# Gathering the next expert unit's rows ahead of sending the finished unit's rows, in a fused attention and mixture-of-experts block

## The chip, the cores and the metric

The kernel is one launch on 1 core of a Trainium2 chip. The metric is device time in microseconds, the median of several executions. The profile shows one execution; in it PE is the TensorE matmul, PEld its weight load, DVE is VectorE, ACT is ScalarE, POOL is GpSimd and SP is SyncE, which here only issues DMAs.

## What is computed

Sixteen sequences of 100 tokens, each of 512 numbers, go through a gated cross-attention with a causal mask and then through a layer of 8 experts, of which each token uses one:

```python
x = x + tanh(g_xattn[0]) * attention(layernorm(x), ctx_512, Wq, Wkv_expand, Wout)
xn = layernorm(x).reshape(-1, 512)
route = sigmoid(xn @ router_w)
max_ind, max_prob = argmax(route, axis=1), max(route, axis=1)
for e in range(8):
    h = silu(xn @ gate_w[e]) * (xn @ up_w[e])
    y = y + where(max_ind == e, h @ down_w[e], 0.0)
x = x + tanh(g_ffn[0]) * (y * max_prob)
```

`gate_w` and `up_w` are 8 x 512 x 1024, `down_w` is 8 x 1024 x 512, all float32. Each float32 product is made of three matmuls on split operands (high part times high part, low times high, high times low).

## The kernel before, in words

The program is written engine by engine: each engine has a block of its own with a fixed order of instructions, and semaphores tie the blocks together. Nothing reorders an engine's instructions; a wait holds up all that stands behind it on that engine.

The first half (up to about 265 us) is attention, in four chunks of 400 tokens, with the routing of each chunk's tokens. It leaves three tables in HBM: `x2_rows`, the normalised rows that the experts read; `x1_rows`, the rows before the expert layer with each token's scale beside them; and `token_table`, which lists for each expert which tokens are its own.

The second half is the expert loop. Its step is a *unit*: up to 256 tokens (`CAP`) of one expert. In the profiled execution there are 8 units, numbered 0 to 7, one for each expert. For one unit:

- GpSimd reads the unit's token numbers from `token_table` into `idx_next` and gathers those rows of `x2_rows` into the tile `xg` by two indirect DMAs of 128 rows (`gather_next`, lines 541 to 546, with the gathers themselves in `gather_tokens`, line 536). `xg` is the memory of the tile `x2`, so the trace shows it as "x<-x_rows,idx_next".
- PE turns the rows (`turn_tokens`, transposes on line 1401: 8 matmuls for a unit) into PSUM, ACT and DVE split them into `x_hi` and `x_lo`. DVE's `x_lo` step counts up the semaphore `g_lo_done`.
- The width of 1024 is worked on in four steps (j from 0 to 3). In each, `gate_up` makes 48 matmuls of 256 columns and `down` 12 of 512 columns (the lines of all of them are 1147 to 1149, the three products of the helper `three`; a gate or up matmul is named "bank<-x_hi,gu_hi" and a down matmul "bank<-wq_hi,wkv_hi", since those buffers are used again).
- SP loads each step's weights (line 407, three DMAs of 512 KB for gate, up and down) into `staging`, which has room for two steps; ACT makes the high parts (`gu_hi`, line 611), DVE the low parts (`gu_lo`, line 780), into buffers for two steps.
- GpSimd reads the token numbers again, into `idx_now`, and gathers the rows of `x1_rows` (`gather_now`, lines 548 to 556). DVE scales the experts' result and adds it to these rows (`finish`, line 1116, tile `rows`, shown as "xn"; semaphore `rows_done`).
- GpSimd scatters the rows to the output (`send_rows`, line 562) with the indices in `idx_now`, and `wait_sent` waits until they have landed before `gather_now` may write `idx_now` anew.

PE's order sets the frame. In its loop iteration u it does gate_up(u,1), down(u,0), gate_up(u,2), down(u,1), turn_tokens(u+1), gate_up(u,3), down(u,2), gate_up(u+1,0), down(u,3). `turn_tokens(u+1)` waits for the gather of unit u+1. DVE does the split of unit u+1's tokens after gate_up(u,3), and `finish(u)` after its step for gate_up(u+1,0).

GpSimd's order in iteration u is send_rows(u), gather_next(u+2), wait_sent(u), gather_now(u+1). So the rows of unit u+2 are asked for when unit u is finished. Before it loads the indices, `gather_next(.., u+2)` waits until `g_lo_done` says that unit u+1's tokens are split, since `xg` has one buffer. `gather_next` for unit 1 stands ahead of the loop; the loop covers units 2 to 7, which is six gathers.

Of the kernel before, what the change touches and what calls it, by code (L numbers as in the profile page):

```python
# [71 lines left out]
def flamingo_block(nc, x, ctx, g_xattn, g_ffn, Wq, Wkv, Wout, router_w, gate_w, up_w, down_w, out):  # L72
    B, S, H = x.shape
    L = ctx.shape[2]
    E, _, I = gate_w.shape
    HD = 32
    NH = H // HD
# [35 lines left out]
    with st:  # L113
# [313 lines left out]
        def _(pool):  # L427
# [106 lines left out]
            def gather_tokens(u):  # L534
                for t in range(TT):
                    nc.gpsimd.indirect_dma_start(xg[:, t, :], None, x2_rows,
                                                 bass.IndirectOffsetOnAxis(ap=idx_next[:, t:t + 1], axis=0),
                                                 bounds_check=T - 1, oob_is_err=False).then_inc(xg_loaded.sem, 16)

            def gather_next(base, u):  # L540
                pool.wait_ge(g_lo_done.sem, g_lo_done.after(u, 0))
                nc.gpsimd.dma_start(idx_next[:], token_table[bass.ds(base, CAP), :].rearrange("(p t) o -> p (t o)", p=P)
                                    ).then_inc(idx_next_loaded.sem, 16)
                pool.wait_ge(idx_next_loaded.sem, idx_next_loaded.after(u - 1, 16))
                pool.sem_inc(wait_passed, 1)
                gather_tokens(u)

            def gather_now(base, u):
                nc.gpsimd.dma_start(idx_now[:], token_table[bass.ds(base, CAP), :].rearrange("(p t) o -> p (t o)", p=P)
                                    ).then_inc(idx_now_loaded.sem, 16)  # L550
                pool.wait_ge(idx_now_loaded.sem, idx_now_loaded.after(u, 16))
                pool.sem_inc(wait_passed, 1)
                for t in range(TT):
                    nc.gpsimd.indirect_dma_start(x1g[:, t, :], None, x1_rows,
                                                 bass.IndirectOffsetOnAxis(ap=idx_now[:, t:t + 1], axis=0),
                                                 bounds_check=T - 1, oob_is_err=False).then_inc(x1g_loaded.sem, 16)

            def send_rows(u):
                for t in range(TT):
                    pool.wait_ge(rows_done.sem, rows_done.after(u, t + 1))  # L560
                    pool.sem_inc(wait_passed, 1)
                    nc.gpsimd.indirect_dma_start(of, bass.IndirectOffsetOnAxis(ap=idx_now[:, t:t + 1], axis=0),  # L562
                                                 rows[:, t, :], None, bounds_check=T - 1,
                                                 oob_is_err=False).then_inc(rows_sent.sem, 16)

            def wait_sent(u):
                pool.wait_ge(rows_sent.sem, rows_sent.after(u, 16 * TT))
                pool.sem_inc(unit_sent.sem, 1)

            def first_slot(u):  # L570
                return pool.value_load(units[0:1, bass.ds(u * 2 + 1, 1)], min_val=0, max_val=slot_max)
# [21 lines left out]
            gather_next(first_slot(1), 1)  # L593
            gather_now(0, 0)
            with pool.Fori(0, more + (E - 2)) as u:
                send_rows(u)
                gather_next(first_slot(u + 2), u + 2)
                wait_sent(u)
                gather_now(first_slot(u + 1), u + 1)
            last = more + (E - 1)  # L600
# [880 lines left out]
```

## Time and profile before

| what | value |
|---|---|
| times of three executions | 595.16, 594.67, 589.15 us; median 594.67 |
| span of the profiled execution, first to last instruction | 593.0 us; its own device time isn't listed apart from the three times above |
| busy share of the span | PE 89%, PEld 75%, DVE 60%, ACT 52%, POOL 31% |
| granted TensorE clock, mean | 0.952 of full speed |
| DMA | 77.31 MB, 130 GB/s on average |

How to read it: the span is shorter than a device time, because what lies before the first and behind the last instruction isn't in it. The ends of matmuls are modelled, so that one matmul's shown duration overlaps the start of the next; the distance from one start to the next is the better measure of what it costs. "[2.33 <-DMA ...]" behind a row is the idle time of that engine before it and what ended it.

### The profile page before, as it was taken

What the parts mean: (1) busy time and instruction counts of PE and PEld (TensorE: products, weight loads), DVE (VectorE), ACT (ScalarE), POOL (GpSimd) and SP (SyncE); (2) the same over time, 40 slices, a digit from 0 to 9 for tenths busy, and PEclk for the clock granted to TensorE, in tenths of its full rate; (3) what the DMA queues carried; (4) which work ended last, traced back from release to release, by engine and by line L of the source; (5) the groups of instructions that cost most, each with busy time, mean ns of one, the idle gap of its engine ahead of it and who ended that gap; (6) DMA issues with size and microseconds to landing.
All of it is one profiled execution on the core that took longest, in us unless ns stands there. A gap on an engine that the chain in (4) does not pass through costs nothing.

```text
span 593.0 us, 11407 instructions
## 1 busy us (share of the span) xinstructions
PE 527.9 (89%) x3724; PEld 446.4 (75%) x3724; DVE 354.3 (60%) x745; ACT 307.5 (52%) x855; POOL 181.1 (31%) x210
## 2 busy tenths in 40 slices
PE   1999999999899999765999899898997997989991
PEld 1966786587658765555899799797997997979981
DVE  3677579557855576873557557475464563755641
ACT  1898659745974795221445535355353443544520
POOL 5544226315631463325311213112124041121111
PEclk9999999999999999955999999999898998999996
DMA  8400121221120310724475656657377366474620
GB/s 208 141 1 2 52 75 58 70 78 48 43 69 14 85 53 21 257 83 99 136 240 176 218 176 213 228 173 222 113 240 249 122 186 225 156 224 134 239 65 27
DMA packets 58910, 77.31 MB, mean 130 GB/s; under 512 B 5398, under 2 KB 40830, under 8 KB 58880
## 3 DMA queue, kind: packets, MB, share of 16 engines
q1 hardware_dynamic: 53728, 66.90, 36.2%
q0 software_dynamic: 5152, 10.03, 5.5%
q8 instruction: 15, 0.25, 0.2%
q14 instruction: 15, 0.12, 0.1%
HBM read 68.81 MB, written 10.86 MB: 134 GB/s over the span
## 4 chain that ended last, share of the span: by engine, by line
PE 51%; DMA 13%; issue 11%; DVE 8%; ACT 7%; POOL 5%; POOLq 2%; DVEq 1%; ACTq 0%; SPq 0%
PE bank L1147 13%; PE bank L1148 13%; PE bank L1149 13%; DMA x<-x_rows,idx_next 7%; DMA idx_next<-token_table 4%; ACT pr L667 3%; POOL pn L507 2%; PE bank L1242 2%; PE bank L1232 2%; PE bank L1401 2%; POOL out_x L562 2%; DMA staging<-in_L_xattn_Wq 2%; PE bank L1281 1%; ACT wq_hi L611 1%; PE bank L1168 1%
## 5 line engine op out<-in xcount | busy, mean ns | idle before, releaser
L1147 PE MATMUL bank<-x_hi,gu_hi 128*128 128x256 f32 x512 | 147.8, 289 | 2.9 <-ACT qT L743 1.5
L1148 PE MATMUL bank<-x_lo,gu_hi 128*128 128x256 f32 x512 | 147.2, 288 | 0.0
L1149 PE MATMUL bank<-x_hi,gu_lo 128*128 128x256 f32 x512 | 146.9, 287 | 0.0
L1147 PEld LDWEIGHTS bank<-x_hi,gu_hi 128*128 128x128 f32 x512 | 100.4, 196 | 4.3 <-DVE x_lo L780 1.8
L1148 PEld LDWEIGHTS bank<-x_lo,gu_hi 128*128 128x128 f32 x512 | 99.8, 195 | 0.8
L1149 PEld LDWEIGHTS bank<-x_hi,gu_lo 128*128 128x128 f32 x512 | 100.1, 196 | 0.0
L667 ACT ACTIVATE pr<-bank,nmx 100x100 f32<-100x100 f32 x256 | 85.6, 376 | 15.5 <-DVE nmx L960 12.1
L780 DVE TENSOR_TENSOR gu_lo<-staging,gu_hi 128x1024 fp32r<-128x1024 f32 x64 | 76.2, 1221 | 10.8 <-ACT gu_hi L611 9.9
L507 POOL TENSOR_TENSOR pn<-pr,inv 100x400 f32<-100x400 f32 x64 | 54.6, 852 | 78.1 <-DVE inv L953 72.9
L611 ACT ACTIVATE gu_hi<-staging 128x1024 fp32r<-128x1024 f32 x64 | 65.5, 1050 | 16.4 <-DMA staging<-in_L_ffn_gate_w 9.2
L562 POOL DMA_INDIRECT out_x<-xn,idx_now x16 | 21.2, 1327 | 145.8 <-DVE xn L1116 143.4
L667 ACT ACTIVATION_READ_ACCUMULATOR pr<-bank,nmx 100x1 f32 x256 | 61.0, 240 | 0.0
L743 ACT ACTIVATE qT<-bank 128x512 f32<-128x512 f32 x32 | 19.2, 599 | 78.1 <-PE bank L1149 78.1
L1232 PE MATMUL bank<-staging,qT 128*100 128x400 f32 x128 | 53.5, 499 | 0.0
L1100 DVE TENSOR_TENSOR qT<-qT,bank 128x512 f32<-128x512 f32 x32 | 21.9, 686 | 49.6 <-ACT qT L743 45.3
L1147 PE MATMUL bank<-wq_hi,wkv_hi 128*128 128x512 f32 x128 | 50.8, 397 | 0.3 <-DVE wq_lo L780 0.3
L1149 PE MATMUL bank<-wq_hi,wkv_lo 128*128 128x512 f32 x128 | 50.4, 393 | 0.0
L1148 PE MATMUL bank<-wq_lo,wkv_hi 128*128 128x512 f32 x128 | 49.9, 390 | 0.0
L960 DVE TENSOR_REDUCE nmx<-bank 100x4 f32<-100x400 f32 x64 | 36.1, 564 | 19.7 <-PE bank L1232 18.9
L611 ACT ACTIVATE x_hi<-bank 128x400 fp32r<-128x400 f32 (+1 forms) x32 | 16.7, 558 | 56.3 <-PE bank L1149 44.1
L780 DVE TENSOR_TENSOR x_lo<-bank,x_hi 128x400 fp32r<-128x400 f32 (+1 forms) x32 | 19.2, 626 | 42.6 <-ACT x_hi L611 42.6
L969 DVE COPY pT<-bank 100x400 f32<-100x400 f32 x64 | 36.3, 567 | 13.4 <-PE bank L1242 12.9
(182 smaller groups left out, 1008.4 us busy)
## 6 DMA issues: line engine op xcount, KB each, us to landing
staging<-in_L_ffn_gate_w SPq DMA_DIRECT2D x32, 512.0 KB, 5.0
staging<-in_L_ffn_up_w SPq DMA_DIRECT2D x32, 512.0 KB, 6.4
staging<-in_L_ffn_down_w SPq DMA_DIRECT2D x32, 512.0 KB
x_rows<-x SPq DMA_DIRECT2D x8, 800.0 KB
xt<-in_x SPq DMA_DIRECT2D x4, 800.0 KB
xr<-in_x SPq DMA_DIRECT2D x16, 200.0 KB
staging<-in_L_xattn_Wq SPq DMA_DIRECT2D x1, 1024.0 KB, 10.6
x<-in_L_xattn_Wout SPq DMA_DIRECT2D x1, 1024.0 KB, 9.3
```

The costliest lines, as they stand in the source:

```text
L507: nc.gpsimd.tensor_tensor(pn[0:S, n % DEEP], pr[0:S, n % 2], inv[0:S, n % DEEP].unsqueeze(2).to_broadcast([S, HP, S]), ALU.mult).then_inc( ...
L562: nc.gpsimd.indirect_dma_start(of, bass.IndirectOffsetOnAxis(ap=idx_now[:, t:t + 1], axis=0), rows[:, t, :], None, bounds_check=T - 1, oob ...
L611: return nc.scalar.activation(dst, src, ACT.Copy)
L667: ins = nc.scalar.activation(pr[0:S, n % 2, h, :], score_b[n % DEEP][0:S, h * S:(h + 1) * S], ACT.Exp, bias=nmx[0:S, n % DEEP, h:h + 1], a ...
L780: return nc.vector.tensor_tensor(dst, src, hi.bitcast(F32), ALU.subtract)
L960: nc.vector.tensor_reduce(nmx[0:S, b], score_b[b][0:S, 0:HP * S].rearrange("p (h s) -> p h s", h=HP), AX.X, ALU.max, negate=True).then_inc ...
L969: nc.vector.tensor_copy(pT[0:S, m % KEEP], turn_b[m % 2][0:S, 0:HP * S].rearrange("p (h s) -> p h s", h=HP)).then_inc(pT_copied.sem, 1)
L1100: nc.vector.tensor_tensor(h_f, silu_g, up_b[j % 2][:].rearrange("p (a n) -> p a n", a=2), ALU.mult).then_inc(h_done.sem, 1)
L1147: nc.tensor.matmul(dst, a[0], b[0], start=first, stop=False)
L1148: nc.tensor.matmul(dst, a[0], b[1], start=False, stop=False)
L1149: return nc.tensor.matmul(dst, a[1], b[0], start=False, stop=last)
L1232: nc.tensor.matmul(score_b[b][0:S, 0:HP * S], qT[:, m, i * S:(i + 1) * S], keys_b[:, m, i].rearrange("p j s -> p (j s)"), start=False, sto ...
```

## The change

In GpSimd's part of the expert loop one call changes its place: `gather_next` for unit u+2 stands at the head of the iteration, before `send_rows(u)`, and no longer between `send_rows(u)` and `wait_sent(u)`. Everything else, the waits included, is as it was; the other engines' instructions are the same.

```diff
@@ -593,8 +593,8 @@
             gather_next(first_slot(1), 1)
             gather_now(0, 0)
             with pool.Fori(0, more + (E - 2)) as u:
+                gather_next(first_slot(u + 2), u + 2)
                 send_rows(u)
-                gather_next(first_slot(u + 2), u + 2)
                 wait_sent(u)
                 gather_now(first_slot(u + 1), u + 1)
             last = more + (E - 1)
```

On GpSimd, at the head of the loop, this stood in the program before (`rows_done` is counted up by DVE's `finish`, `g_lo_done` by DVE's split of the tokens; `out_x` is the output, `x<-x_rows,idx_next` the gather of the rows):

```order
L562 DMA out_x<-xn,idx_now 1600x512 [waits rows_done]
L560 REGISTER_ALU
L562 DMA out_x<-xn,idx_now 1600x512 [waits rows_done]
L571 ISA
L571 TENSOR_LOAD units
L571 ISA x2
L541 REGISTER_ALU
L542 REGISTER_ALU [waits g_lo_done]
L542 DMA idx_next<-token_table 128x2
L544 ISA
L536 DMA x<-x_rows,idx_next 128x512 [waits idx_next_loaded]
L536 DMA x<-x_rows,idx_next 128x512
```

And this stands there now, at the same place of the same engine:

```order
L541 REGISTER_ALU
L542 REGISTER_ALU [waits g_lo_done]
L542 DMA idx_next<-token_table 128x2
L544 ISA
L536 DMA x<-x_rows,idx_next 128x512 [waits idx_next_loaded]
L536 DMA x<-x_rows,idx_next 128x512
L560 ISA
L562 DMA out_x<-xn,idx_now 1600x512 [waits rows_done]
L560 REGISTER_ALU
L562 DMA out_x<-xn,idx_now 1600x512 [waits rows_done]
```

The index load and the two gathers have moved ahead of both scatters, so that they no longer stand behind the two waits for `rows_done`; the scatters now stand behind the waits for `g_lo_done` and `idx_next_loaded`.

## Rows read from the trace of the kernel before

**Rows 1.** The page: the chain that ended last, shares of the span by engine.

```profile
PE 51%; DMA 13%; issue 11%; DVE 8%; ACT 7%; POOL 5%; POOLq 2%; DVEq 1%; ACTq 0%; SPq 0%
```

**Rows 2.** Waits of PE, 335 to 593 us: total us, times, longest.

```profile
PE bank L1401 <- DMA x<-x_rows,idx_next: 16.2, 6, 3.1
PE bank L1147 <- DVE wq_lo L780: 0.3, 1, 0.3
```

**Rows 3.** Timeline of PE: start, us, line, tile, count, idle before.

```profile
302.01 1.03 PE L1401 MATMUL bank<-ident,x 128*128 128x128 f32 x8
...
336.20 0.39 PE L1148 MATMUL bank<-wq_lo,wkv_hi 128*128 128x512 f32 x1
336.43 0.39 PE L1149 MATMUL bank<-wq_hi,wkv_lo 128*128 128x512 f32 x1
339.15 1.09 PE L1401 MATMUL bank<-ident,x 128*128 128x128 f32 x8 [2.33 <-DMA x<-x_rows,idx_next]
...
376.39 1.09 PE L1401 MATMUL bank<-ident,x 128*128 128x128 f32 x8 [2.39 <-DMA x<-x_rows,idx_next]
...
414.01 1.96 PE L1401 MATMUL bank<-ident,x 128*128 128x128 f32 x8 [2.79 <-DMA x<-x_rows,idx_next]
...
454.72 1.96 PE L1401 MATMUL bank<-ident,x 128*128 128x128 f32 x8 [3.14 <-DMA x<-x_rows,idx_next]
...
493.99 1.09 PE L1401 MATMUL bank<-ident,x 128*128 128x128 f32 x8 [3.06 <-DMA x<-x_rows,idx_next]
...
532.87 1.96 PE L1401 MATMUL bank<-ident,x 128*128 128x128 f32 x8 [2.51 <-DMA x<-x_rows,idx_next]
```

**Rows 4.** Stretches of PE: length, busy (instructions), granted clock, DMA share, GB/s.

```profile
302.01:336.66 34.65, 34.65 (x249) 1.00 0.65 204
414.01:451.58 37.57, 37.57 (x248) 0.92 0.56 187
...
493.99:530.36 36.37, 36.37 (x248) 0.95 0.59 188
532.87:536.30 3.43, 3.43 (x17) 0.52 0.87 293
```

**Rows 5.** Timeline of GpSimd around one unit's end.

```profile
399.45 1.00 POOL L562 DMA_INDIRECT out_x<-xn,idx_now  x1 [0.30 <-issue]
400.44 0.61 POOL L542 DMA_DIRECT2D idx_next<-token_table  x1
405.21 1.31 POOL L536 DMA_INDIRECT x<-x_rows,idx_next  x1 [4.17 <-DMA idx_next<-token_table]
406.83 1.01 POOL L536 DMA_INDIRECT x<-x_rows,idx_next  x1 [0.30 <-issue]
...
437.77 1.75 POOL L562 DMA_INDIRECT out_x<-xn,idx_now  x1 [20.34 <-DVE xn L1116]
```

**Rows 6.** Timelines of DVE, SP, ACT and PE in the same unit.

```profile
383.87 1.29 DVE L780 TENSOR_TENSOR x_lo<-bank,x_hi 128x512 fp32r<-128x512 f32 x2 [4.19 <-ACT x_hi L611]
...
389.41 0.37 SPq L407 DMA_DIRECT2D staging<-in_L_ffn_gate_w  x1
...
394.44 2.11 ACT L611 ACTIVATE gu_hi<-staging 128x1024 fp32r<-128x1024 f32 x2
...
397.03 2.35 DVE L780 TENSOR_TENSOR gu_lo<-staging,gu_hi 128x1024 fp32r<-128x1024 f32 x2
...
402.61 0.28 PE L1147 MATMUL bank<-x_hi,gu_hi 128*128 128x256 f32 x1
```

**Rows 7.** Timelines of SP and ACT: a weight load issued beside the gather.

```profile
369.02 0.39 SPq L407 DMA_DIRECT2D staging<-in_L_ffn_gate_w  x1
...
376.05 1.06 ACT L611 ACTIVATE gu_hi<-staging 128x1024 fp32r<-128x1024 f32 x1 [1.85 <-DMA staging<-in_L_ffn_gate_w]
```

**Rows 8.** The page's DMA issues: count, KB each, median us to landing.

```profile
staging<-in_L_ffn_gate_w SPq DMA_DIRECT2D x32, 512.0 KB, 5.0
```

## The prediction

> **What bounds the kernel now.** I read the page first. Its chain of work that ended last is half PE, with DMA next at 13% and GpSimd at 5% [rows 1]. In a kernel whose weights are loaded far ahead, DMA and GpSimd on the chain call for a question: which transfer is PE waiting for? The waits of PE over the expert loop answer it. There are six waits for one thing, the gathered rows of the next unit, 16.2 us in all, and beside them one wait of 0.3 us [rows 2]. So nothing else stops PE in this half: it runs its queue without a gap, then stands still once a unit in front of the transposes on line 1401.
>
> The timeline of PE gives the size [rows 3]. Transposes start at 302.01 without a wait (that gather was asked for ahead of the loop), and then at 339.15, 376.39, 414.01, 454.72, 493.99 and 532.87, each after 2.3 to 3.1 us of idling. The work of one unit at full clock is read between the first two: the last matmul in front of the wait starts at 336.43, and one of its kind follows its predecessor after 0.23 us (336.20 to 336.43), so the transposes could have started at 336.66. That is 34.65 us after 302.01, in a stretch that is all busy at clock 1.00 [rows 4].
>
> Two units later the price of waiting shows a second time. After the waits at 414.01, 493.99 and 532.87 the granted clock of the following stretches is below 1.00 [rows 4]; right behind the last it is 0.52 over 3.4 us, which is the 1.2 GHz level. Behind 302.01, where PE had not idled, it stayed at 1.00. The same eight transposes take 1.09 us at the high clock and 1.96 at the low one. So each wait costs its own length and, in most units, some work at half speed after it.
>
> Why is the gather late? GpSimd sends the finished rows (second scatter at 399.45), only then issues the index load at 400.44, gathers at 405.21 and 406.83, and PE can go on at 414.01, 7.2 us after the second gather [rows 3, 5]. That whole string of 13.6 us hangs on `rows_done`, which has nothing to do with it.
>
> **The change part by part.** It moves one index load, two gathers and their waits ahead of the two scatters, six times (units 2 to 7). No instruction is added or removed, and no other engine's order changes.
>
> *When the gather happens now.* It is bound to `g_lo_done`, the split of the preceding unit's tokens, which DVE ends at 383.87 + 1.29 = 385.16 in the unit shown [rows 6]. GpSimd is idle at that time: it waits some 17 to 22 us a unit for finished rows (20.3 in the next one) [rows 5]. The index load is then issued at about 385.3. From index load to first gather it is 405.21 - 400.44 = 4.8 us, to the second 6.4, and to PE's start 13.6 [rows 3, 5]. So the rows are there at about 398.9. PE would want them at 376.39 + 34.65 = 411.04. That is 12 us of slack where there were about 3 us missing; even a gather twice as slow would be in time. I count the six waits as gone entirely.
>
> *The gain.* From the first transposes to the last it is 532.87 - 302.01 = 230.86 us for six units [rows 3]. Six units at 34.65 are 207.90. The difference is 22.96 us. Of this the idle time is 16.2 us (17.2 counted from start to start, since the shown ends of matmuls reach 0.17 us too far), and the remaining 5.7 us is work done at the low clock in three of the units. Behind 532.87 the clock is low for another 3.43 us at 0.52, which costs 3.43 x 0.48 = 1.6 us [rows 4]. Together 24.6 us.
>
> The TensorE part of this is where the Trainium skill can be weighed. The rows come first: four of the six waits are followed by stretches at a reduced clock, and two (before 339.15 and 376.39) are not [rows 3, 4]. "TensorE: Matmul & The Clock Gate" (section "What's actually happening") says that throttled is the default state and activity releases it; taken by itself this gives back the whole 7.3 us of low clock once PE never idles, and a clock that had nothing to do with the waits would leave only 17.2 us. The trace sides with the page: in no stretch of the loop without a preceding wait is the clock below 1.00.
>
> *What stands behind the new waits.* The scatters of unit u now stand behind the wait for `g_lo_done`. That wait has ended at 385.2, while the first rows are done only after 395.7, and GpSimd is through with the second gather at about 385.3 + 6.4 + 1.0 = 392.7. So `send_rows` starts when it does today. If that cover were gone, the scatter would be late by the difference, and its readers (the reuse of `rows` one unit later) have 30 us to spare. `wait_sent` today is over before GpSimd gets there, since the gather stands between; now GpSimd sits in it. A scatter should land about as fast as the gather, 5 to 7 us, so the load of `idx_now` is issued at 400.4 + 5 to 7 = 405 to 408, against 407.8 today [rows 5]. Its rows are needed at about 436: cost nothing.
>
> *What is issued beside the gather now.* This is the one real price. Today the gather at 405 to 408 (and its likes) stands beside a weight load whose delay is seen: the one issued at 369.02 is taken by ACT at 376.05 after a wait of 1.85 us, 7.0 us where the median landing is 5.0 [rows 7, 8]. It does not reach PE. In its new place, with first gather at about 390.1, it stands beside the gate and up loads of step 2 (389.41) [rows 6]. Let the same 2 us, and 1 us because SP's issue stands behind GpSimd's, fall on it: ACT starts on it at 397.4 in place of 394.44, is done with the gate half at 398.5, DVE has its low part at 399.7. PE wants it at 402.61 [rows 6]. Slack 2.9 us; the up half has 2.8 us more of PE work in front of it. Cost taken: nothing. The lower bound is a gain of nothing too (the old neighbour of the gather gets its load sooner, but it had slack). The upper bound: if the load were late by 7 us and not 3, PE would wait 1.1 us a unit, 6.6 us in all, and again lose some clock, at most the 7.3 us of today.
>
> The traffic mix is where another rule bears on it. The row is the 7.0 us load beside a gather [rows 7]. "DMA: Bandwidth & Descriptors" (section "SWDGE vs HWDGE vs iDMA") says that loads issued by SP and gathers issued by GpSimd enter different queues in each DMA engine, which takes them in turn. By that rule the weight load would share with the gather and be delayed by about its bytes, not stand behind all of it. The trace agrees as far as one 7.0 us landing can tell.
>
> **The sum.** The profile's span of 593.0 would become 568.4. Its own device time isn't given; I put the 1.7 us between span and median around it, so 594.67 - 24.6 = 570.1 us. The three times spread over 6 us (589.15 to 595.16), which is the size of the clock term in the loop; the fastest run may have had almost none. From that run only the idling would go, 589.15 - 17.2 = 571.9, which fits.
>
> **The rivals.**
> - *Waits go, but the new neighbour costs.* The weight load beside the moved gather is late enough to reach PE by about a microsecond a unit, and the clock falls now and then again. For it: two 512 KB loads and the gather are in flight at once. Against it: 2.9 us of slack over a delay already counted. Time: 570.1 + 6.6, and a part of the clock term, up to 579.
> - *The clock isn't tied to the waits.* Only the 17.2 us go: 577.5. Against it: the stretch from 302.01 at 1.00.
> - *It doesn't do what it says.* `g_lo_done` would have to come so late that the gather is no earlier, or GpSimd be busy until `rows_done`. Against it: 385.16 and the 20 us of idling. Time 594.7.
> - *Slower.* One mechanism: the gather's descriptors get in front of the gate load and hold it up for long. PE loses its present 2.9 us of wait and gets it back at step 2. From about 3 us of new wait plus the slack used up, that is a load 10 us late or 15 us from issue to landing, three times the median of 5.0 [rows 8], the kernel is slower. At 11 us late it is about 1 us a unit, 601 us. Nothing in the trace comes near that.
>
> **How the numbers follow.** The forecast of 570 has 0.80; a costly neighbour (574 to 579) 0.10; the untied clock 0.04; no effect 0.03; slower 0.03. The range must leave out no more than 2 in 10: downwards to 565, for a median run that had more clock loss than the profiled one, upwards to 578 for both middle rivals. About 1% is what a measurement of this kernel can tell from no change. Faster by more than that: 0.80 + 0.10 + 0.04 = 0.94. Within 1%: 0.03. Slower: 0.03.
>
> **What would show it right or wrong.** In the profile of the changed kernel the wait of PE for "x<-x_rows,idx_next" in the loop should be left with the one ahead of unit 0 only. The transposes should start every 34.65 us, at 1.09 us for the eight, with clock 1.00 from 302 to about 580. GpSimd's first gather should come about 5 us after the `x_lo` split, before its scatters, and GpSimd should show a wait of some 5 us for the scatter's landing. ACT's wait for the gate weights should have moved from the step behind the transposes to step 2 of the next unit. A wait of PE on `gu_lo` would mean the costly neighbour; transposes at distances over 35 us without any wait would mean that the clock is on its own. The forecast is wrong if the time is above 578 or if PE still waits for the rows.

## The result and the profile after

| kernel | median us | lowest to highest | executions |
|---|---|---|---|
| before | 594.54 | 589.15 to 595.16 | 4 |
| changed | 570.12 | 568.93 to 571.81 | 4 |

The medians lie 24.4 us apart, which is a quotient of 0.959. The recorded ratio is 0.9662, 95% interval 0.9612 to 0.9711, a gain of 17 to 23 us with 20 in the middle. What sets it apart from the medians I can't say; the gains measured later beside the kernel before (21.3 us by e1, 20.3 by e5) lie on the side of the ratio. The forecast was 570, with 24.6 us of gain. Executions of the kernel before that took over 1.5% more than its fastest are left out of all ratios and gains. The profiled execution of the changed kernel took 570.18 us at a span of 568.7 us, so 1.5 us lie around the span.

The chain of work that ended last, shares by engine, from the page of the changed kernel (answers to [rows 1]):

```profile
PE 72%; DVE 7%; issue 6%; ACT 5%; POOL 3%; DMA 2%; DVEq 0%; ACTq 0%; SPq 0%; POOLq 0%
```

DMA fell from 13% to 2% and PE rose from 51% to 72%: from 302 to 550 us the chain no longer leaves PE. The waits of PE from 290 to 570 us (total us, times, longest), which answer to [rows 2]:

```profile
PE bank L1147 <- DVE wq_lo L780: 0.3, 1, 0.3
```

The six waits for the rows are gone; the 0.3 us near the end is the same as before. The timeline of PE at the transposes (start, us, line, tile, count), answering to [rows 3]:

```profile
302.47 1.04 PE L1401 MATMUL bank<-ident,x 128*128 128x128 f32 x8
...
337.11 1.04 PE L1401 MATMUL bank<-ident,x 128*128 128x128 f32 x8
...
371.72 1.04 PE L1401 MATMUL bank<-ident,x 128*128 128x128 f32 x8
...
406.33 1.04 PE L1401 MATMUL bank<-ident,x 128*128 128x128 f32 x8
...
510.15 1.04 PE L1401 MATMUL bank<-ident,x 128*128 128x128 f32 x8
```

They come every 34.6 us, and none shows idling before it. And two stretches of PE (length, busy, granted clock, DMA share, GB/s), answering to [rows 4]:

```profile
302.47:510.15 207.68, 207.68 (x1490) 1.00 0.67 217
510.15:513.60 3.45, 3.45 (x32) 1.00 0.71 211
```

PE is busy through all six units, at clock 1.00. Between the two profiled executions the 24.3 us of span come from three places: the six units took 207.68 us in place of 230.86 (23.2 less), what lies behind the last transposes took 568.7 - 510.15 = 58.55 in place of 593.0 - 532.87 = 60.13 (1.6 less), and the part ahead of the loop was 0.5 us longer, which no edit explains.

GpSimd over one iteration of the changed kernel, answering to [rows 5]:

```profile
381.08 0.59 POOL L542 DMA_DIRECT2D idx_next<-token_table  x1 [4.73 <-DVE x_lo L780]
383.94 2.01 POOL L536 DMA_INDIRECT x<-x_rows,idx_next  x1 [2.27 <-DMA idx_next<-token_table]
386.26 1.00 POOL L536 DMA_INDIRECT x<-x_rows,idx_next  x1 [0.31 <-issue]
392.67 1.75 POOL L562 DMA_INDIRECT out_x<-xn,idx_now  x1 [5.41 <-DVE xn L1116]
394.73 1.01 POOL L562 DMA_INDIRECT out_x<-xn,idx_now  x1 [0.30 <-issue]
400.64 0.58 POOL L549 DMA_DIRECT2D idx_now<-token_table  x1 [4.91 <-issue]
```

The index load is released by the `x_lo` split, both gathers are issued by 387.3, and GpSimd then idles 5.4 us until the first finished rows: the scatter isn't late. The 4.91 us before the `idx_now` load, for which the profile names no releaser, stand where the program has `wait_sent`: they are the wait for the scatter's landing, which the gather had covered before. From index load to first gather it is now 2.9 us, where it was 4.8 [rows 5].

The neighbours of the moved gather, in the timelines of ACT, DVE, PE and SP of the changed kernel (answering to [rows 6] and [rows 7]):

```profile
358.76 1.06 ACT L611 ACTIVATE gu_hi<-staging 128x1024 fp32r<-128x1024 f32 x1 [2.62 <-DMA staging<-in_L_ffn_up_w]
359.86 1.22 DVE L780 TENSOR_TENSOR gu_lo<-staging,gu_hi 128x1024 fp32r<-128x1024 f32 x1 [0.95 <-ACT gu_hi L611]
363.27 0.28 PE L1147 MATMUL bank<-x_hi,gu_hi 128*128 128x256 f32 x1
...
384.06 0.37 SPq L407 DMA_DIRECT2D staging<-in_L_ffn_down_w  x1
384.68 0.37 SPq L407 DMA_DIRECT2D staging<-in_L_ffn_gate_w  x1
...
389.71 1.04 ACT L611 ACTIVATE gu_hi<-staging 128x1024 fp32r<-128x1024 f32 x1
391.32 1.06 ACT L611 ACTIVATE gu_hi<-staging 128x1024 fp32r<-128x1024 f32 x1 [0.56 <-DMA staging<-in_L_ffn_up_w]
392.30 2.35 DVE L780 TENSOR_TENSOR gu_lo<-staging,gu_hi 128x1024 fp32r<-128x1024 f32 x2
397.88 0.28 PE L1147 MATMUL bank<-x_hi,gu_hi 128*128 128x256 f32 x1
...
399.66 2.35 DVE L780 TENSOR_TENSOR gu_lo<-staging,gu_hi 128x1024 fp32r<-128x1024 f32 x2
399.90 0.37 SPq L407 DMA_DIRECT2D staging<-in_L_ffn_down_w  x1
401.50 0.39 SPq L407 DMA_DIRECT2D staging<-in_L_ffn_gate_w  x1
407.38 1.06 ACT L611 ACTIVATE gu_hi<-staging 128x1024 fp32r<-128x1024 f32 x1 [0.69 <-DMA staging<-in_L_ffn_gate_w]
```

At step 2 of the unit from 371.72 on, ACT waits 0.56 us for the up weights, and not at all for the gate weights. DVE ends that pair at 394.65, and the first of the two is wanted by PE at 397.88: over 3 us of room. This unit has the shortest of the six waits. Over the six units they are 0.8, 2.6, 0.6, 0.9, 1.8 and 1.8 us, 1.4 in the mean, all for the up weights; the kernel before has two waits of 0.3 us at this step. The longest (358.76) lets DVE end at 361.08, still 2.2 us before PE begins the step at 363.27.

The gate load that goes out beside the moved gather (384.68, the gather at 383.94) follows 0.6 us behind its down load: SP isn't held up there. The gate load at 401.50 still follows 1.6 us behind, though no gather stands beside it any more.

### The profile page after: what moved, and what is told of

Read it like the earlier page. It is cut to its first block, busy times and chain, and to the rows that moved or that the text cites. A ratio compares the mean times of both kernels' runs of the same rounds, so it can differ in the third digit from the quotient of the medians.

```text
span 568.7 us, 11407 instructions
## 1 busy us (share of the span) xinstructions
PE 519.9 (91%) x3724; PEld 439.8 (77%) x3724; DVE 355.4 (63%) x745; ACT 308.1 (54%) x855; POOL 184.4 (32%) x210
## 4 chain that ended last, share of the span: by engine, by line
PE 72%; DVE 7%; issue 6%; ACT 5%; POOL 3%; DMA 2%; DVEq 0%; ACTq 0%; SPq 0%; POOLq 0%
PE bank L1147 20%; PE bank L1149 20%; PE bank L1148 20%; ACT pr L667 3%; POOL pn L507 3%; PE bank L1242 2%; PE bank L1232 2%; DMA staging<-in_L_xattn_Wq 2%; PE bank L1281 1%; PE bank L1401 1%; PE bank L1168 1%; PE bank L1251 1%; ACT staging L611 1%; PE bank L1289 1%; DVE pT L969 1%
## 5 line engine op out<-in xcount | busy, mean ns | idle before, releaser
L1147 PE MATMUL bank<-x_hi,gu_hi 128*128 128x256 f32 x512 | 145.2, 284 | 2.5 <-DVE x_lo L780 1.4
L1148 PE MATMUL bank<-x_lo,gu_hi 128*128 128x256 f32 x512 | 144.8, 283 | 0.0
L1149 PE MATMUL bank<-x_hi,gu_lo 128*128 128x256 f32 x512 | 144.8, 283 | 0.0
L1147 PEld LDWEIGHTS bank<-x_hi,gu_hi 128*128 128x128 f32 x512 | 97.8, 191 | 4.0 <-DVE x_lo L780 1.8
L1148 PEld LDWEIGHTS bank<-x_lo,gu_hi 128*128 128x128 f32 x512 | 97.4, 190 | 0.8
L1149 PEld LDWEIGHTS bank<-x_hi,gu_lo 128*128 128x128 f32 x512 | 97.8, 191 | 0.0
L667 ACT ACTIVATION_READ_ACCUMULATOR pr<-bank,nmx 100x1 f32 x256 | 59.8, 235 | 0.0
L780 DVE TENSOR_TENSOR wq_lo<-staging,wq_hi 128x1024 fp32r<-128x1024 f32 x32 | 39.3, 1227 | 8.2 <-ACT wq_hi L611 8.2
L1242 PEld LDWEIGHTS bank<-ident,pn 100*100 100x100 f32 x256 | 24.4, 128 | 20.7 <-POOL pn L507 8.6
```

Source lines behind the costliest of these rows:

```text
L667: ins = nc.scalar.activation(pr[0:S, n % 2, h, :], score_b[n % DEEP][0:S, h * S:(h + 1) * S], ACT.Exp, bias=nmx[0:S, n % DEEP, h:h + 1], a ...
L780: return nc.vector.tensor_tensor(dst, src, hi.bitcast(F32), ALU.subtract)
L1147: nc.tensor.matmul(dst, a[0], b[0], start=first, stop=False)
L1148: nc.tensor.matmul(dst, a[0], b[1], start=False, stop=False)
L1149: return nc.tensor.matmul(dst, a[1], b[0], start=False, stop=last)
L1242: ins = nc.tensor.transpose(turn_b[n % 2][0:S, h * S:(h + 1) * S], pn[0:S, n % DEEP, h, :], ident[0:S, 0:S])
```

## The experiments

My theory: PE stood still in front of the transposes because the gather hung on the finished rows, and the stretches at the low clock followed from that standing still; both parts together are the gain, and nothing else is. Rivals: the clock falls by itself; the gain comes from less traffic beside the weight loads; the moved gather costs something at its new place. The runs e1 to e4 were made on one chip and e5 to e8 on another occasion, each group beside runs of the kernel before: 590.72 us (586.55 to 595.71, 13 executions) with the first and 593.04 us (587.26 to 598.71, 11 executions) with the second.

### e1: only the index load moved

```diff
             with pool.Fori(0, more + (E - 2)) as u:
-                gather_next(first_slot(u + 2), u + 2)
+                load_next(first_slot(u + 2), u + 2)
                 send_rows(u)
+                gather_loaded(u + 2)
                 wait_sent(u)
```

`load_next` waits for `g_lo_done` and issues the index load, `gather_loaded` waits for its landing and issues the two gathers.

> Half of the change: only the index load of unit u+2 (with its wait for the token split) stands ahead of the scatters; the two gathers stand behind them, as before. My theory (the six waits of PE for the rows, and the low clock behind them, are all that the change removed): the load's 4.8 us leave the string that hangs on rows_done, and some 3 us were missing, so PE should wait no more or by under 0.5 us a unit, and the time should be 570 to 574 us. Rival A (the gathers themselves have to be far ahead, since they collide with the weight loads at the old place): part of the gain only, 578 to 590. Rival B (the gain is something else in the order): near 594.

Measured: 569.40 us (568.93 to 570.12), ratio to before 0.9643 (0.9579 to 0.9706): all of the gain. GpSimd in one iteration:

```profile
379.82 0.58 POOL L542 DMA_DIRECT2D idx_next<-token_table  x1 [6.88 <-DVE x_lo L787]
391.42 1.74 POOL L568 DMA_INDIRECT out_x<-xn,idx_now  x1 [11.02 <-DVE xn L1123]
393.47 1.00 POOL L568 DMA_INDIRECT out_x<-xn,idx_now  x1 [0.30 <-issue]
394.78 1.04 POOL L536 DMA_INDIRECT x<-x_rows,idx_next  x1 [0.31 <-issue]
396.12 1.01 POOL L536 DMA_INDIRECT x<-x_rows,idx_next  x1 [0.30 <-issue]
```

Counted from the unit's first transposes, the gathers come some 12 us later than in the changed kernel, still behind both scatters, and PE starts its next transposes at 405.07 without idling. So it isn't the early place of the gathers that pays. The string was about 3 us too long, and taking one link out of it was enough. Rivals A and B fall.

### e2: the kernel before, with PE kept busy while it waits

```diff
-            def turn_tokens(u):
-                pe.wait_ge(xg_loaded.sem, xg_loaded.after(u, 16 * TT))
+            def turn_tokens(u, fill=0):
                 pe.wait_ge(g_lo_done.sem, g_lo_done.after(u, 0))
+                for _ in range(fill):
+                    nc.tensor.matmul(xT_b[0][:], wo_hi[:, 0, 0:P], wo_hi[:, 0, :], start=True, stop=True)
+                pe.wait_ge(xg_loaded.sem, xg_loaded.after(u, 16 * TT))
...
-                turn_tokens(u + 1)
+                turn_tokens(u + 1, 10)
```

> The kernel before, with ten idle matmuls of 512 columns (0.23 us each, 2.3 us together) that PE does in the six units' (and unit 1's) place of waiting, ahead of the wait for the gathered rows; they write to a bank that the transposes then overwrite. The rows arrive as late as before. My theory (the low clock follows from PE's idling): PE still loses the 17.2 us but none of the 7.3 us of low clock, all stretches of the loop at 1.00; 587.3 us plus up to 2.3 for unit 1, whose rows are there in time, so 587 to 590. Rival (the clock falls by itself, for other reasons than idling): reduced stretches stay, 594 to 597.

Measured: 588.12 us (586.53 to 590.09, 10 executions), ratio to before 0.9971 (0.9938 to 1.0003). PE at one unit, and its stretch over the six units:

```profile
449.32 2.43 PE L1399 MATMUL bank<-wo_hi 128*128 128x512 f32 x10
452.98 1.09 PE L1403 MATMUL bank<-ident,x 128*128 128x128 f32 x8 [1.23 <-DMA x<-x_rows,idx_next]
```

```profile
302.96:528.00 225.04, 223.25 (x1555) 1.00 0.62 199
```

The transposes are held up as long as in the kernel before: the six units take 225.04 us, 17.1 more than six times 34.65, where the kernel before stands still for 17.2. Yet the clock is 1.00 over all six units, where the kernel before has 0.97 from 302 to 535. (Only before two of the six units does PE still wait for the rows behind its idle matmuls, 0.3 and 1.2 us; before the others the 2.3 us of matmuls fill the whole wait.) That is what tells the two theories apart: with the standing still replaced by work that nobody needs, the low clock is gone.

As to time, 588.12 less the 2.3 us of idle matmuls at unit 1, which had no wait, is 585.8. The kernel before at a clock of 1.00 in the loop should take about that; it took 590.72 beside these runs, so I estimate its loss to the low clock at 4.9 us in the median. The interval of the ratio reaches 1.0003, so by time alone this would not be settled. The clock decides it, and not only in the one trace: the mean clock of all ten executions lies between 0.966 and 0.971, that of the 13 executions of the kernel before between 0.915 and 0.967.

### e3: the changed kernel, with PE made to wait for rows it doesn't need

```diff
                 pe.wait_ge(xg_loaded.sem, xg_loaded.after(u, 16 * TT))
                 pe.wait_ge(g_lo_done.sem, g_lo_done.after(u, 0))
+                if not isinstance(u, int):
+                    pe.wait_ge(x1g_loaded.sem, x1g_loaded.after(u - 1, 16 * TT))
```

> The changed kernel, in which PE, ahead of the transposes of unit v, also waits for the x1 rows of unit v-1, which it does not need there. Its own rows lie ready. My theory: these rows land about 5 us after 406.6 where PE wants to go on at 406.3, so PE idles some 5 to 6 us a unit seven times, each followed by work at the low clock (1.7 us), 45 to 55 us in all: 610 to 625 us. If the clock were not tied to the idling: 603 to 608, with stretches at 1.00. Rival (what the change removed was the collision of the gather with weight loads, not the standing still): near 570, PE making the time up.

Measured: 623.17 us (2 executions, 621.76 and 624.58), ratio to before 1.0549 (1.0455 to 1.0642). The waits of PE, and two stretches of 5 us behind one of them:

```profile
PE bank L1403 <- DMA x<-x_rows,idx_now: 33.0, 7, 10.1
```

```profile
425.00:430.00 5.00, 1.71 (x9) 0.81 0.70 201
430.00:435.00 5.00, 5.00 (x25) 0.51 0.79 270
```

The time is 53 us above that of the changed kernel (570.12, measured on another occasion). Between the two profiled executions the span is 51.5 us longer: 33.0 are the seven waits, 13.0 the low clock over the six units, 2.5 the low clock behind the last wait, and 3 lie ahead of the loop, where this execution also shows the wait described under e5. The first wait is 1.3 us and the clock behind it stays at 1.00; the six others are 3.3 to 10.1 us, and over the 5 us behind each the clock is 0.50 to 0.53. That is the mirror of e2. The needed rows lie ready and no traffic is added, and the time is lost all the same, because PE stands still.

The waits were expected at 5 to 6 us each and scatter more widely. The one of 10.1 us follows on an index load that took 6.4 us to its gather (issued at 503.03), where the other six took 4.0 to 5.4, and on rows that were there 5.5 us behind the last gather and not 2.4 to 4.7. Why those transfers were slower is open.

### e4: three times the gather traffic at the new place

```diff
+            def gather_extra():
+                for k in range(4):
+                    nc.gpsimd.indirect_dma_start(xt[:, k, :], None, x2_rows,
+                                                 bass.IndirectOffsetOnAxis(ap=idx_next[:, k % TT:k % TT + 1], axis=0),
+                                                 bounds_check=T - 1, oob_is_err=False).then_inc(extra_loaded.sem, 16)
...
             with pool.Fori(0, more + (E - 2)) as u:
+                pool.wait_ge(extra_loaded.sem, extra_loaded.after(u + 1, 0))
                 gather_next(first_slot(u + 2), u + 2)
+                gather_extra()
                 send_rows(u)
```

> The changed kernel with four more gathers of 128 rows behind the two of each unit, into a tile that nobody reads: three times the gather traffic beside the weight loads of step 2, and GpSimd busy until about the time when the first rows are done. My theory (ACT and DVE have over 4 us to spare there): ACT's wait for the weights of step 2 grows from 0.6 to 2 to 4 us, PE waits at most 0.5 us a unit, 570 to 574 us. Rival, the costly neighbour: PE waits for gu_lo by 1 us or more a unit and the clock falls here and there, 578 to 590.

Measured: 570.65 us (2 executions, 570.49 and 570.81), ratio to before 0.966 (0.9578 to 0.9742). The waits of ACT for weights from 300 to 560 us, first of the changed kernel, then of this one:

```profile
ACT gu_hi L611 <- DMA staging<-in_L_ffn_up_w: 10.6, 12, 2.6
ACT gu_hi L611 <- DMA staging<-in_L_ffn_gate_w: 4.3, 6, 1.1
```

```profile
ACT gu_hi L621 <- DMA staging<-in_L_ffn_up_w: 16.2, 18, 2.1
ACT gu_hi L621 <- DMA staging<-in_L_ffn_gate_w: 9.9, 11, 1.7
```

ACT's waits grow from 14.9 to 26.1 us, and none of it reaches PE: it has no wait on the split weights in the loop beyond the known 0.3 us, and its six units take 207.68 us as in the changed kernel. The costly neighbour falls, with room to spare. My expectation for ACT was wrong in its place: the waits of step 2 don't grow at all (1.4 us in the mean, as in the changed kernel, where I had said 2 to 4). The whole growth lies one step later, where the weights of step 3 are loaded beside the added gathers; no single wait is over 2.1 us.

### e5: the changed kernel once more, beside the kernel before

> The changed kernel once more, beside the kernel before on the same chip. The kernel before has by now taken 586.6 to 595.7 us, and my theory has a reason: its low clock behind the waits comes in some executions more, in some less, between 0 and 7 us; the changed kernel never idles in the loop and has no such part. So: changed 569 to 571 with a spread under 3 us, before 586 to 596, gain 19 to 25 us in the mean, ratio 0.960 to 0.968. Rival (the changed kernel has its clock loss too, only seldom): single executions of it above 574.

Measured: 572.01 us (570.46 to 573.96); ratio 0.9657 (0.9611 to 0.9702), 20.3 us less. The time is above the 569 to 571 that I expected, the spread is 3.5 us and not under 3, and the highest is just under 574. Of the 11 executions of the kernel before, the fastest (587.26) has a mean clock of 0.966 and the slowest (598.71) one of 0.951: time goes with clock, as the theory says. One of the 13 executions beside e1 to e4 doesn't fit (590.72 us at 0.915); there is no trace of it.

The profiled execution is the slowest of the six, and it shows a thing that the first profile had not: PE waits 2.0 us ahead of unit 0's step 1, and the clock is down afterwards. (In the first profile the wait at this place was 1.1 us, and the clock stayed at 1.00.)

```profile
287.74 0.38 PE L1147 MATMUL bank<-x_hi,gu_hi 128*128 128x256 f32 x1 [1.99 <-issue]
```

```profile
287.74:290.00 2.26, 2.26 (x15) 0.78 0.00 0
290.00:295.00 5.00, 5.00 (x35) 0.76 0.79 246
```

### e6: the gather later still

```diff
             with pool.Fori(0, more + (E - 2)) as u:
                 send_rows(u)
-                gather_next(first_slot(u + 2), u + 2)
                 wait_sent(u)
                 gather_now(first_slot(u + 1), u + 1)
+                gather_next(first_slot(u + 2), u + 2)
```

> The opposite of the change: in the kernel before, the index load and gathers of unit u+2 stand behind the gather of x1 rows for unit u+1 too, the last thing of the iteration. My theory (the time is PE's string: rows done, GpSimd's queue, gather, transposes): the string gets longer by the scatter's landing (5 us) and by index load and gather of the x1 rows (7 us), 12 to 14 us a unit six times, and clock loss behind every wait: 660 to 685 us. Rival (PE's waits are an effect of traffic, whatever the order): below 620.

Measured: 662.96 us (2 executions, 659.94 and 665.98), ratio 1.1199 (1.1103 to 1.1296).

```profile
PE bank L1401 <- DMA x<-x_rows,idx_next: 73.6, 6, 14.1
```

Six waits of 12.3 us in the mean where there had been six of 2.7: the string got longer by 9.6 us, somewhat less than the 12 to 14 expected. Between the two profiled executions the span grew by 65.4 us (593.0 to 658.4). Of these 57.4 are the waits, 3.5 lie ahead of the loop, where this execution has a wait of 2.3 us like that of e5, and the remaining 4.5 are mostly work at the low clock, whose mean falls to 0.88 between 305 and 620. Each microsecond put into the string comes out at the end, with a small extra charge.

### e7: the wait in front of the loop on an earlier signal

The same line in the programs of ACT, DVE and PE; here PE's. The changed order of GpSimd stands.

```diff
-            pe.wait_ge(units_loaded, 16)
+            pe.wait_ge(rows_known, 1)
             more = pe.value_load(more_units[0:1, 0:1], min_val=0, max_val=UNITS_MAX - E)
```

> The changed kernel, in which PE, ACT and DVE wait for rows_known and not for units_loaded before they read the number of units: they need only that number, which DVE wrote, and not the table that GpSimd loads. In the trace PE idles 0 to 1.4 us at 285. My theory: up to 1 us gained, 568.5 to 570. Rival: something else ends PE's wait there, no difference.

Measured: 567.48 us (566.47 to 567.96), beside 572.01 (570.46 to 573.96) for the changed kernel on the same chip; ratio to before 0.9584 (0.9524 to 0.9644). The two don't overlap: 4.5 us, four times the 1 us I had allowed. From unit 0's transposes to unit 1's, first in e5, then in e7:

```profile
274.54:306.23 31.69, 28.28 (x177) 0.83 0.54 136
```

```profile
271.64:299.62 27.98, 26.57 (x176) 0.86 0.60 161
```

3.7 us less. 2.0 are the wait, and the rest is again the low clock that followed it. I had counted only the wait, and from a profile in which it was short. The comparison flatters e7, since the profiled execution of e5 is its slowest. Against the first profile of the changed kernel, whose wait there was 1.1 us without a lower clock behind it, the same stretch (29.6 us there) is 1.6 us shorter. e7 is the fastest kernel of this study and beats both kernels of the case.

### e8: PE kept busy in front of unit 0 as well

The file has the changed order of GpSimd and the edit of e7; the filler of e2 stands only in front of unit 0:

```diff
-            turn_tokens(0)
+            turn_tokens(0, 15)
```

> The kernel before with two things added in front of the loop, and without the change of order (so it stands beside the kernel before, not the changed one): 15 idle matmuls of PE ahead of the wait for unit 0's rows, where it idles 6.4 us at the low clock, and the wait for rows_known as in the run with that alone. If this file holds the changed order, the base is 570. My theory (the clock follows what PE did before): the stretch from 272 to 281 runs at 1.00, unit 0's first gate and up matmuls take 5.7 and not 8 us and its transposes 1.0 and not 2.0, about 3 us gained over the changed order, 566 to 568. Rival (DVE and ACT, which split the weights and rows of unit 0, bound this stretch): under 1 us gained.

Measured: 569.39 us (567.93 to 569.91), ratio to before 0.9622 (0.9562 to 0.9681). Against e7 (567.48) nothing is gained; it is 1.9 us slower. The same stretch from unit 0's to unit 1's transposes, then PE where its work starts, then 5 us of it:

```profile
273.39:300.26 26.87, 25.30 (x177) 0.94 0.60 164
```

```profile
273.39 1.09 PE L1403 MATMUL bank<-ident,x 128*128 128x128 f32 x8 [1.55 <-DMA x<-x_rows,idx_next]
276.06 0.39 PE L1147 MATMUL bank<-x_hi,gu_hi 128*128 128x256 f32 x1 [1.57 <-DVE x_lo L780]
```

```profile
275.00:280.00 5.00, 3.94 (x20) 0.66 0.71 166
```

The transposes ran at the high clock (1.09 us), so the filler did its part, but PE had waited 1.55 us for the rows in front of them, and 1.1 us of work later it waits 1.57 us for their split, and the clock falls again. The stretch is 1.1 us shorter than in e7, and the start of it came 1.75 us later. The filler itself didn't hold PE up there, since PE still waited for the rows behind it; whether the later rows are chance or due to the filler in another way stays open. The 3 us that I had expected are not there.

## Why the prediction was right

**What bounds the kernel.** Right. That PE works without a gap at 34.65 us a unit, save for the wait for the rows, was read from [rows 3] and [rows 4]; the changed kernel runs all six units at 34.6, in its two profiles as in those of e1 and e4.

**The string that hangs on `rows_done`.** Right, and shown from both sides: shorter by the index load alone, PE doesn't wait (e1); longer by the scatter's landing and the index load and gather of the `x1_rows`, PE waits 9.6 us more a unit (e6).

**The gain in two terms.** Between the two profiled executions the terms are as forecast: 22.96 us over the six units against 23.2 measured, 1.6 behind them against 1.6. But the second term, the low clock, is not a constant of the kernel. I took 7.3 us of it from one profiled execution, and that execution was a typical one on that chip. Beside e1 to e4 the kernel before loses an estimated 4.9 us to it in the median (e2), and the gain there was 21.3 us by e1; beside e5 it was 20.3. So the forecast of the time is right because the changed kernel has no such term in the loop (570.12, 572.01), while the gain of 24.6 us is at the upper end of what was measured, 20.3 to 24.4, and above the interval of the recorded ratio (17 to 23). That 570 and 570.12 meet so closely is luck: single executions of the changed kernel range from 568.9 to 574.0. The prediction had seen the 6 us spread of the three times and named the clock as its reason; it should have drawn from that a range for the gain, not only for the time.

That the clock follows the standing still was argued from six waits and one stretch without a wait, and the rival had 0.04. Now it is shown: e2 takes the low clock away and leaves the lateness, e3 brings the waits and the low clock back and leaves the rows early. "TensorE: Matmul & The Clock Gate" (the Trainium skill, section "What's actually happening"), which ties the clock to PE's activity, agrees with both.

**What stands behind the new waits.** Right. GpSimd idles 5.4 us ahead of the first scatter, and the wait for the landing is 4.9 us where 5 to 7 were said.

**The costly neighbour.** The mechanism was placed right and somewhat overpriced. I put 3 us on the weight loads of step 2: 2 by analogy with [rows 7] and 1 for SP's issue standing behind GpSimd's. Measured are waits of 0.6 to 2.6 us, 1.4 in the mean, so the 2 us were of the right size. The one microsecond was a wrong reading: beside the moved gather SP's loads go out 0.6 us apart. SP's gate load comes 1.6 us behind the down load in the changed kernel too, where no gather is near: it waits for DVE's `gu_lo` (started at 399.66, 1.2 us for each of the two), which frees the staging buffer. And ACT's waits for the gate weights behind the transposes, one of which is the 1.85 us of [rows 7], are still there in part with the gather gone (4.2 us over the six units, where there were 8.1), so they were not the gather's alone. The sign that this wait would move to the gate weights of step 2 came only in part: half of it stayed, and what came up at step 2 is a wait for the up weights. Nothing hung on it, since even 3 us were covered, and e4 shows that three times the traffic is covered too.

**The index load.** Its 4.8 us were carried over from [rows 5] to the new place. It took 2.8 to 2.9 us there in all six units, where the kernel before has 4.5 to 5.3. The same stretch in both kernels, from the index load to the first gather, first before, then changed (length, busy, clock, DMA share, GB/s):

```profile
400.40:405.20 4.80, 4.80 (x33) 1.00 0.55 193
381.10:383.90 2.80, 2.80 (x26) 1.00 0.03 6
```

The load of 1 KB now goes out in a lull. The load of `idx_now` in the changed kernel, just as large, speaks for this too: it takes 4.4 to 6.0 us in these units, at a DMA share of 0.66 to 0.82, and 3.4 at 0.37 behind them (539.94). That is an argument, not a test; no run changed the traffic around an index load alone.

## What to carry to other kernels

When an engine that issues DMAs in order has two jobs, look for the one that waits on late work and for the one that doesn't need it, and ask how many microseconds the second is short: here 3 us were missing, and moving one small index load was as good as moving the whole gather. Price a wait of PE by its length and by the low clock behind it, but take the second part as a range over several executions, not from one profile. A wait of PE for a signal that comes later than what it needs is worth a look even at 1 to 2 us.

## What the runs showed of the hardware that I had not expected

- Short waits of PE of like length are followed by a lower clock in one case and not in the next. In [rows 3] 2.33 and 2.39 us were not followed by slow transposes and 2.51 us was. Ahead of unit 0's step 1, waits of 1.0 to 1.5 us (both kernels' first profiles, e2, e4) left the clock at 1.00, and those of 1.99 us (e5), 1.96 (e3) and 2.29 (e6) were followed by 0.66 to 0.69 over the next 3 to 4 us. In e8 two waits of 1.55 and 1.57 us, 1.1 us of work apart, were followed by 0.57 over 3.9 us.
- The kernel before takes 586.6 to 598.7 us from one execution to the next, and its time goes with its mean clock. The changed kernel, whose loop stands at clock 1.00 in both its profiles, spans 568.9 to 574.0.
- The same 1 KB index load lets the gather start after 2.8 to 2.9 us at a DMA share of 0.03 or less, and after 4.5 to 5.3 us at 0.55 to 0.62.
